# Graph attention on one core: Q·K per head in one VectorE instruction, one head of V on GpSimd

## What is computed

```python
edge_index = jnp.stack([src, dst])
rows, cols = (edge_index[0], edge_index[1])
q = (x @ Wq + bq).reshape(n, H, DK)          # x is layer-normed
k = (x @ Wk + bk).reshape(n, H, DK)
v = (x @ Wv + bv).reshape(n, H, DK)
logits = jnp.einsum('ehd,ehd->eh', q[rows] * scale, k[cols]) + att_bias
row_max = jax.ops.segment_max(logits, rows, num_segments=n)
p = jnp.exp(logits - row_max[rows])
denom = jax.ops.segment_sum(p, rows, num_segments=n)
att = p / denom[rows]
y = jax.ops.segment_sum(att[:, :, None] * v[cols], rows, num_segments=n)
out = y.reshape(n, H * DK) @ Wo + bo
```

## Time and profile before

| | |
|---|---|
| median of three runs | 3326.24 us (3325.85 to 3329.14) |
| profiled execution: span | 3328.5 us |
| profiled execution: its time | as its span, within the three timed ones |
| DVE busy over the span | 2900.1 us (87%), 8850 instructions |
| PE, ACT, POOL busy | 2913.6 (88%), 2181.1 (66%), 2204.1 us (66%) |
| tile loop, first to last `pr` | 1161.1 to 2931.5 us |

### The profile page before, as it was taken

The page is one execution under the profiler, slowest core; times in us unless marked ns, Lnnn a source line. Parts: engine busy times, 40 slices in busy tenths (PEclk is TensorE's granted clock), DMA queues, the critical chain, the costliest instruction groups (busy, mean ns, idle before and its releaser), DMA issues.

```text
span 3328.5 us, 51387 instructions
## 1 busy us (share of the span) xinstructions
PE 2913.6 (88%) x11922; PEld 1712.5 (51%) x12048; DVE 2900.1 (87%) x8850; ACT 2181.1 (66%) x7642; POOL 2204.1 (66%) x2509
## 2 busy tenths in 40 slices
PE   6897889887988169999999999999999999989999
PEld 4554445554554025555555555555555555555555
DVE  9897777776776279999999999999999999998886
ACT  6432222222221039999999999999999999964443
POOL 0377777777777647777777777777777777741111
PEclk9898888888888589999999999999999999999998
DMA  6344333333332487888888888788888888831221
GB/s 209 80 136 107 106 99 103 103 106 100 103 103 85 166 286 256 255 253 254 257 256 260 253 261 253 254 255 256 255 256 255 260 253 258 256 100 66 76 76 69
DMA packets 259197, 615.22 MB, mean 185 GB/s; under 512 B 69755, under 2 KB 80327, under 8 KB 258642
## 3 DMA queue, kind: packets, MB, share of 16 engines
q0 software_dynamic: 144832, 443.72, 42.3%
q1 hardware_dynamic: 107718, 155.40, 15.5%
q10 hardware_dynamic: 6348, 12.80, 1.1%
HBM read 550.28 MB, written 61.49 MB: 184 GB/s over the span
## 4 chain that ended last, share of the span: by engine, by line
DVE 28%; POOL 25%; issue 20%; PE 15%; DMA 8%; DVEq 2%; another core or an unknown queue 1%; ACT 0%; ACTq 0%; SPq 0%; POOLq 0%
POOL rec_scratch L631 21%; DMA big<-kv_scratch,small 8%; DVE big L1396 7%; DVE small L1289 6%; DVE big L1283 5%; PE banks L1920 5%; POOL big L652 2%; PE banks L1899 2%; PE banks L1982 2%; DVE big L1009 2%; PE banks L1847 1%; POOL small L659 1%; PE banks L1755 1%; DVE big L1014 1%
## 5 line engine op out<-in xcount | busy, mean ns | idle before, releaser
L815 ACT ACTIVATE big<-big,small 128x65 f32<-128x65 f32 x6564 | 1604.3, 338 | 4.8
L652 POOL DMA_INDIRECT big<-kv_scratch,small x832 | 842.3, 1012 | 407.6 <-DVE small L1289 286.5
L631 POOL DMA_INDIRECT rec_scratch<-big,small x782 | 770.6, 985 | 342.2 <-issue 237.7
L1899 PE MATMUL banks<-big,small 128*128 128x260 f32 x3328 | 897.9, 393 | 87.0 <-POOL small L659 45.6
L1847 PE MATMUL banks<-big,small 128*128 x1664 | 873.3, 607 | 34.6 <-DVE big L1283 16.1
L1899 PEld LDWEIGHTS banks<-big,small 128*128 128x128 f32 x3328 | 598.8, 190 | 522.3 <-issue 249.7
L1755 PE MATMUL banks<-big 128*128 128x512 f32 (+1 forms) x1176 | 611.1, 668 | 22.3 <-DVE big L999 22.3
L1396 DVE SCALAR_TENSOR_TENSOR big<-big,loS,banks 128x520 f32 x832 | 611.5, 735 | 5.4 <-PE banks L1899 4.4
L1283 DVE TENSOR_TENSOR big<-banks,big 128x512 f32<-128x512 f32 x832 | 558.8, 672 | 44.7 <-PE banks L1847 24.1
L659 POOL TENSOR_SCALAR small<-iotaF,small 128x128 f32<-128x128 f32 x832 | 525.9, 632 | 50.6 <-PE banks L1899 25.1
L1289 DVE TENSOR_REDUCE small<-big 128x8 f32<-128x512 f32 x832 | 548.8, 664 | 0.0
(11 more groups left out here) (263 smaller groups left out, 2720.4 us busy)
## 6 DMA issues: line engine op xcount, KB each, us to landing
rowR<-lo_rows SPq DMA_DIRECT2D x97, 256.0 KB
big<-src_rows SPq DMA_DIRECT2D x97, 256.0 KB, 3.5
big<-in_x_dram SPq DMA_DIRECT2D x96, 256.0 KB, 2.8
big<-kv_scratch,small POOLq DMA_INDIRECT x832, 5.2
rec_scratch<-big,small POOLq DMA_INDIRECT x782
kv_scratch<-big SPq DMA_DIRECT2D x48, 260.0 KB
q_scratch<-big SPq DMA_DIRECT2D x48, 256.0 KB
kv_scratch<-big SPq DMA_DIRECT2D x48, 256.0 KB
```

What stands on the lines that cost most here:

```text
L631: e.indirect_dma_start(recd, bass.IndirectOffsetOnAxis(ap=ridx[:, c % 4, j:j + 1], axis=0), rec[:, 8 * c + j, :], None).then_inc(s_sc[c % ...
L652: e.indirect_dma_start(KV[:, vat(t):vat(t) + YW + D], None, KVd, bass.IndirectOffsetOnAxis(ap=recB[b_ % 4][:, t % 16, 9:10].bitcast(i32), ...
L815: ins = e.activation(heads(Vr(t), h, h + 1), heads(Vr(t), h, h + 1), ACT.Copy, scale=ph[:, h:h + 1])
L1899: ins = e.matmul(YB[t % 2][:, i, :], oh[t % 4], Vr(t)[:, 260 * i:260 * i + 260], start=True, stop=True)
```

## The change

On DVE `pr` and `rd` are replaced by `kq`: eight instructions of 64 numbers per tile, one per head, each of which multiplies and gives the sum through its accumulator output. Four stand where `pr(s)` stood and four where `rd(s-1)` stood; both halves are of tile s. The logits of tile s are so complete one step earlier. The semaphore s_pr goes; what waited for it waits for s_rd, which comes with the eighth head. On POOL a new `pvp` multiplies head 7 of V by p, between `gather(s)` and `one_hot(s-25)`, for tile s-23; it waits for s_ex. ACT does heads 0 to 6. The one-hot of `scale_parts` compares two tensors, where it was a tensor and a scalar per partition.

```diff
-        s_oh, s_q1, s_pr, s_rd, s_lb, s_x2 = sem("s_oh"), sem("s_q1"), sem("s_pr"), sem("s_rd"), sem("s_lb"), sem("s_x2")
+        s_oh, s_q1, s_rd, s_lb, s_x2 = sem("s_oh"), sem("s_q1"), sem("s_rd"), sem("s_lb"), sem("s_x2")
...
         HV = 4
+        HP = 7
+        s_pvp = sem("s_pvp")
...
+            def pvp(t):
+
+                v = Vr(t)[:, 65 * HP:520].rearrange("p (h d) -> p h d", d=65)
+                q.wait_ge(s_kv[t % 8], 16 * (t // 8 + 1))
+                q.wait_ge(s_ex, t // 16 + 1)
+                e.tensor_tensor(v, v, pB[t // 16 % 2][:, t % 16, HP:8].rearrange("p (h a) -> p h a", a=1).broadcast_to([128, 8 - HP, 65]), ALU.mult).then_inc(s_pvp, 1)
...
+                if 0 <= s - DEL < T:
+                    pvp(s - DEL)
                 if s - DEL - 2 >= 0:
                     one_hot(s - DEL - 2)
...
                 q.wait_ge(s_pva, 16 * (b_ - 1))
+                q.wait_ge(s_pvp, 16 * (b_ - 1))
                 e.activation(flat(pB[b_ % 2]), DP, ACT.Exp).then_inc(s_ex, 1)
...
-                for h in range(HV if t >= LAST else 0, 8):
+                for h in range(HV if t >= LAST else 0, HP):
...
-            def pr(t):
+            def kq(t, half):
 
                 q.wait_ge(s_q1, t + 1)
                 q.wait_ge(s_kv[t % 8], 16 * (t // 8 + 1))
-                e.tensor_tensor(Kr(t), QB[t % 2], Kr(t), ALU.mult).then_inc(s_pr, 1)
-
-            def rd(t):
-
-                q.wait_ge(s_pr, t + 1)
                 q.wait_ge(s_x2, t // 16 - 1)
-                e.tensor_reduce(Lr[t // 16 % 2][:, t % 16, :], Kr(t).rearrange("p (h d) -> p h d", d=64), AX.X, ALU.add).then_inc(s_rd, 1)
+                for h in range(4 * half, 4 * half + 4):
+                    k_ = Kr(t)[:, 64 * h:64 * h + 64]
+                    ins = e.scalar_tensor_tensor(k_, QB[t % 2][:, 64 * h:64 * h + 64], 1.0, k_, ALU.mult, ALU.mult,
+                                                 accum_out=Lr[t // 16 % 2][:, t % 16, h:h + 1])
+                if half:
+                    ins.then_inc(s_rd, 1)
...
-                e.tensor_scalar(Aoh[0:8, :], iotaF[0:8, :], llb[0:8, max(b_ - 1, 0):max(b_ - 1, 0) + 1], None, ALU.is_equal).then_inc(s_bd, 1)
+                e.tensor_tensor(Aoh[0:8, :], iotaF[0:8, :], llb[0:8, max(b_ - 1, 0):max(b_ - 1, 0) + 1].broadcast_to([8, 128]), ALU.is_equal).then_inc(s_bd, 1)
...
                 if s < T:
-                    pr(s)
+                    kq(s, 0)
...
-                if 1 <= s < T and at != 0:
-                    rd(s - 1)
+                if s < T:
+                    kq(s, 1)
...
                 q.wait_ge(s_oh, t // 4 + 1)
-                q.wait_ge(s_pr, t - 1)
+                q.wait_ge(s_rd, t - 1)
                 q.wait_ge(s_q[k], q_base[k] + 16)
...
                 q.wait_ge(s_pva, t + 1)
                 q.wait_ge(s_pvv, t - LAST + 1)
+                q.wait_ge(s_pvp, t + 1)
```

More of the change, by code:

```diff
@@ L582, in _ @@
             q.wait_ge(s_rd, T)
-            q.wait_ge(s_pr, T)
             q.wait_ge(s_q1, T)
@@ L1470, in _ @@
                 t = s - DEL - 3
-                if at == 0:
-                    rd(s - 1)
                 if 0 <= t < T:
@@ L1904, in f_yT @@
                 q.wait_ge(s_yn, w + 1)
-                q.wait_ge(s_pr, T)
+                q.wait_ge(s_rd, T)
                 q.wait_ge(s_yT, w)
```

## The result

| | before | after |
|---|---|---|
| median | 3326.05 us (3318.67 to 3329.14, 4 runs) | 3492.06 us (3487.40 to 3495.95, 4 runs) |
| ratio | | 1.0499, interval 1.0483 to 1.0514 |
| profiled span | 3328.5 us | 3494.1 us |
| loop, first to last `pr` / `kq` | 1770.4 us | 1942.0 us (1161.0 to 3103.0) |
| DVE, PE, ACT, POOL busy, share of the span | 87, 88, 66, 66% | 83, 85, 57, 70% |

A forecast was written before the change was run, and what follows sets the result against it. DVE was taken to bound the kernel, at 33.7 us a block; a ring of waits of 36.0 us would replace it, 2.3 us more in 50 blocks, 115 us on 3328.5: 3441 us, range 3295 to 3585.

The forecast's parts named there:

- the ring: Once-a-block loop from `less` over POOL's `pvp` and late gathers to the next `less`: 8.0 + 15.5 + 12.5 = 36.0 us.
- x: Price of `pvp` on POOL, in no row: 0.35 us taken, between 0.16 and 0.54.
- The way to p: From the start of `less` over `expand_q`, `dt` and `p_exp` to the start of `pvp`: 1.6 us.
- Where the gathers cease to be the bound: Seven POOL turns after `kq(392)`, at `kq(399)`, DVE becomes the slower one again; 12.5 us to the next `less`.
- The count of 50 blocks: Of 52 blocks 50 pay 2.3 us each; the last and the first are left out.
- B: Rival on DVE: each accumulator read costs 0.07 us on top, 41 us a block, 3715 us; chance 0.06.
- C: Rival: POOL is simply full, 16 turns outlast the ring from 0.43 us on; 3561 to 3640 us; chance 0.14.
- D: Rival: it cancels, the ring at a low x equals today's block; within 7 us of now; chance 0.05.
- that for QB's banks: PE's wait until all heads are done: over 2.4 us available for 0.86 us of work, so hidden.
- A: Rival: p comes early enough, DVE stays the bound at 32.2 us a block; 68 us less, 3258 us; chance 0.17.
- forecast saving of 1.3 us a block: DVE's own work: 1.1 us a block from eight heads (1.12 against 1.19 a tile) plus 0.2 from the one-hot.
- The one-hot's 0.2: DVE's block one-hot from two tensors takes 0.20 us instead of 0.41: 0.2 us a block saved.

The follow-up runs named there:

- pvp_only: Kernel before plus only POOL's product of V's head 7, ACT with seven heads, `pr` and `rd` kept: 3488.57 us, ratio 1.0484.
- wait_only: Kernel before plus only a POOL wait for p between gather and one-hot, no work added: 3449.93 us, ratio 1.0363.
- pvp_late: Changed kernel with `pvp` two tiles later, right ahead of the one-hot of the same tile: 3348.96 us, ratio 1.0064.
- late1: Changed kernel with `pvp` one tile later: 3615.76 us on another chip where the kernel before took 3559.78, ratio 1.0154.
- p_early: Changed kernel, in a block's step 6 `p_exp` ahead of ACT's V multiplications and `dt` ahead of `expand_q`: 3658.88 us on the chip with 3559.78 before, ratio 1.0289.
- kq_only: Changed kernel without POOL's part and with the old one-hot, so only `pr` and `rd` are replaced by eight instructions: 3292.72 us, ratio 0.9894.
- heads2: Changed kernel with two heads (6 and 7) in `pvp` and six on ACT: 3743.47 us on the chip with 3559.78 before, ratio 1.0526.
- aoh_only: Kernel before with only the block's one-hot from two tensors: 3326.93 us over 11 runs, ratio 0.9996.

## Why the prediction was right, and where it was not

**The direction and the mechanism held.** The forecast was that `pvp` of a block's first tile stands for `p_exp` on POOL and the next gather stands behind it, so that DVE waits for a late landing. Every sign named for it came: the wait once a block (3.0 us; "2 us or more"), DVE at 90.7% of the stretch ("about 90%"), waits at `kq` from the eighth step on (tile 376 is eight tiles behind 368, the first of block 23), gathers that hardly wait for the reduction, a turn of 2.13 us ("2.2"), eight heads in 1.15 us ("1.12", 2037.41 to 2038.56), `kq(376)` late by 1.39 us ("1.4"). This last one fits in part by luck: gather(376) was issued 3.54 us behind `less` and not 2.8, and its data was used 4.62 us later and not 5.2. `pvp_only`, `wait_only`, `pvp_late` and `late1` show the cause from four sides: the loss is there without the DVE part, is mostly there without any work, is mostly gone when the work stays and the wait goes, and is down to a third when the wait is made shorter by one tile.

**The size was off by 51 us, and the steps that failed are three terms of the ring.** Read once around block 22 from the rows above:

| term | forecast, us | measured, us |
|---|---|---|
| `less` to the start of `pvp` | 1.6 | 2036.54 to 2038.89 = 2.35 |
| `pvp` to the gather behind it | 0.35 + 0.82 = 1.17 | 2038.89 to 2040.08 = 1.19 |
| POOL's turns until DVE is the slower one again | 7 x 2.21 = 15.5 | 9 turns, 2040.08 to 2059.22 = 19.14 |
| issue of the last late gather to its `kq` | 5.2 | 2059.22 to 2064.66 = 5.44 |
| DVE from there to the next `less` | 12.5 | 2064.66 to 2073.54 = 8.88 |
| ring | 36.0 | 37.0 |

- *x.* "I take the middle, 0.35 us": it is 0.27 us start to start. By the forecast's own formula the ring would have been 33.2 + 8 x 0.27 = 35.4 us, so this error hid part of the others: with x right the forecast would have been 3409 us, 83 too low and not 51. That much of the closeness is luck. The estimate from the Trainium skill (GPSIMD Engine Reference, Performance versus the Vector engine), 0.31, was nearer than my middle.
- *The way to p, 2.35 us and not 1.6.* The step was: "It will now sit at `p_exp` and wait for it." ACT did not sit there. `dt` was done at 2037.73 + 0.27 = 2038.00, and `p_exp` began at 2038.50, right behind the second of two multiplications of V (2035.05 to 2038.50, with a small instruction between them) that stand ahead of it in its program. ACT had indeed idled, 2.18 us, but in front of L787, two steps earlier in its program, most likely for PE's product L1865. Free time ahead of an instruction is no free time at the next. The rows for this were in my hands: `p_exp` of the kernel before began at 2002.77 and `less` at 2000.35, 2.42 us apart, and I replaced this measured distance by a sum of hand-overs through an ACT that I took to be free; with it the term would have been 2.72, nearer to 2.35. Of the 0.75 us that were missing, ACT's multiplications make 0.45 (0.50 from `dt`'s end to `p_exp`, forecast 0.05). `expand_q` started 0.23 behind `less` (forecast 0.05), `dt` 0.96 behind that (0.86) and `pvp` 0.14 behind the end of `p_exp` (0.05). `p_early` shows that this way is on the ring: `pvp` started 1.23 us sooner, and 67 us came back, some 1.3 us a block.
- *Where the gathers cease to be the bound.* "From there on the work of the block's end makes DVE the slower one again" was set at the eighth tile behind the border; it is the tenth (tile 385 still waits 0.32 us). Two turns of POOL, 4.26 us, stand in place of 12.5 - 8.88 = 3.6 us of DVE, and from issue to `kq` it took 5.44 us instead of 5.2: together 0.9 us a block.

Corrected, the ring is 35.4 + 0.75 + 0.9 = 37.0 us; the mean over the loop is 37.2. The count of 50 blocks held.

**The rivals.** *B* (short instructions cost more than they show) is refuted by `kq_only`: the eight heads cost 0.144 us each, the accumulator read's 0.07 us start under the next head, and the kernel gains. The estimate of 1.53 us that I took from the Trainium skill (VectorE: DVE Perf Modes, the TRN2 errata) is a third above the 1.15 measured. *C* (POOL full) was not the cause, but it is what holds `pvp_late`. *D* (it cancels) is out with 166 us; even at the low x of 0.16 the ring would be some 36 us, an estimate (37.0 less ten times 0.11). Of the waits that the forecast put at nothing, that for QB's banks stayed there: in `kq_only` no `kq` waits for PE. *A* is `kq_only`: the gain is real, at 33 us, half of its price of 68. Of the forecast saving of 1.3 us a block, 0.65 came (33.7 to 33.05). The one-hot's 0.2 gave nothing measurable, and the heads save 16 x (1.19 - 1.15) = 0.6 us instead of 1.1; about 0.16 us more could come from `pr`'s waits, 5.8 us in 1200, of which 1.1 are left in `kq_only`. That these add up to 0.8 and not 0.65 is within what one block's rows can tell.

**Still open:** why `wait_only` costs 124 us. That the wait makes it is sure; how its 2.6 us a block divide between the later landing, ACT's eight heads on the way to p and the gathers that wait for the reduction was not tested. Nor is it known why `heads2` costs 18 us and not some 34.

## What to carry to other kernels

Before an instruction with a wait is put on an engine that works in order, list what is queued behind it: here POOL idled a fifth of the loop, but was three tiles ahead with loads, and a wait of 3 us once a block took that lead and came back as 3.5 us a block on engines that never touch the new instruction. Place the consumer so late that its data is there: two tiles later gave back 143 of 166 us here, since `yt`, in the same step, holds V's slot that long anyway. Then ask whether the engine that gets relief was the bound at all. For the way to a releaser, take the measured start of the releasing instruction in the old trace, with everything that its engine does first, and not a sum of hand-overs.

## What the runs showed of the hardware

- A product of two tensors on GpSimd took 0.27 us start to start for 65 numbers per partition, 0.38 for 130 (in `heads2`, 2122.03 to 2122.41), 1.26 for 512. From the first two an estimate of the fixed part is 0.16 us, from the first and the last 0.13.
- An accumulator read of 0.07 us behind each product of 64 numbers on DVE costs nothing visible: eight products with reads take 1.15 us, one multiplication of 512 numbers and one reduction of them 1.19.
- The comparison of 8x128 numbers with a scalar per partition took DVE 0.41 us to the next start and 0.73 by its own duration; as a comparison of two tensors 0.21 and 0.27 (`aoh_only`).
- The trace can put a wait down to the wrong releaser: `kq(376)` is booked on PE's product of Q, done 2 us before, where only the gather was still out. And it can miss records: 65 of 129 products of L1865 are not in it, and 65 waits of their reader are booked as "remote".
